# Spreading reciprocals by DMA instead of by matmul, and dividing half of q on GpSimd, in a fused linear-attention and mixture-of-experts kernel

## The reference

```python
qp = _phi(proj(Wq, bq)); kp = _phi(proj(Wk, bk)); v = proj(Wv, bv)     # _phi(x) = elu(x) + 1
# for every token t, in order:
kv   = kv + outer(k_t, v_t)            # per head, 32 x 32
ksum = ksum + k_t                      # per head, 32
num  = q_t @ kv
den  = dot(q_t, ksum) + 1e-6           # one number per token and head
out  = num / den                       # then out @ Wo.T + bo, added to x
```

## Time and profile before

| | us |
|---|---|
| median of 3 runs (lowest to highest) | 1915.71 (1914.94 to 1915.79) |
| the profiled execution, its own time | 1916.06 |
| its span, first to last instruction | 1914.3 |
| PE busy | 1890.7 (99%) |
| weight loads busy, beside PE | 1659.6 (87%) |
| DVE busy | 1569.2 (82%) |
| POOL busy | 889.8 (46%) |
| ACT busy | 663.8 (35%) |
| DMA queue of the program, share of 16 engines | 35.4% |

### The profile page before, as it was taken

One profiled execution on the slowest core, in us unless ns is written; L12 is line 12 of the kernel. 1 busy time (PEld: TensorE's weight loads), 2 busy tenths in 40 slices (PEclk: granted clock), 3 DMA queues, 4 the chain that ended last, 5 costly groups with the idle time before them and its releaser, 6 DMA issues.

```text
span 1914.3 us, 60181 instructions
## 1 busy us (share of the span) xinstructions
PE 1890.7 (99%) x25412; PEld 1659.6 (87%) x25412; DVE 1569.2 (82%) x3356; ACT 663.8 (35%) x1298; POOL 889.8 (46%) x981
## 2 busy tenths in 40 slices
PE   7999999999999999999999999999999999999997
PEld 6888888888888888888888888888888888888887
DVE  7888787888879888778878888887888897888888
ACT  4333333323333332333333433333333333323331
POOL 4345554455443554534554445544345553455422
PEclk9999999999999999999999999999999999999999
DMA  6343234333243432343323334333443234333222
GB/s 215 101 128 112 96 106 128 118 118 112 90 127 119 127 121 74 123 125 116 123 89 118 117 112 136 100 98 113 128 128 112 85 114 130 117 117 113 89 73 90
DMA packets 171197, 217.97 MB, mean 114 GB/s; under 512 B 24368, under 2 KB 85808, under 8 KB 170928
## 3 DMA queue, kind: packets, MB, share of 16 engines
q1 hardware_dynamic: 170928, 214.13, 35.4%
HBM read 151.02 MB, written 63.04 MB: 112 GB/s over the span
## 4 chain that ended last, share of the span: by engine, by line
PE 95%; DVE 2%; POOL 1%; DMA 1%; issue 0%; SPq 0%; ACT 0%; POOLq 0%; DVEq 0%
PE ring L684 38%; PE ring L666 36%; PE ring L758 7%; PE num_ps L788 6%; PE num_ps L771 3%; PE num_ps L801 2%; PE ring L730 1%; PE ring L743 1%; DMA v_tok<-in_wv_t 1%; DVE s_mask L973 0%; PE ring L654 0%; DVE stats L1091 0%; DVE den L1220 0%; DVE res L1084 0%; DVE o_lo L1215 0%
## 5 line engine op out<-in xcount | busy, mean ns | idle before, releaser
L1315 POOL TENSOR_TENSOR k_sum<-k_sum,q_raw 128x512 f32<-128x512 f32 x128 | 165.3, 1291 | 545.0 <-DVE q_raw L984 545.0
L883 ACT ACTIVATE e_tmp<-ring,bias_n 128x512 f32<-128x512 f32 x256 | 175.9, 687 | 509.3 <-PE ring L666 508.7
L973 DVE TENSOR_TENSOR s_mask<-ring,causal 128x512 f32<-128x512 f32 x512 | 315.0, 677 | 0.0
L684 PE MATMUL ring<-wv_hi,xt_hi 128*128 128x260 f32 x1024 | 298.9, 292 | 0.0
L684 PE MATMUL ring<-wv_hi,xt_lo 128*128 128x260 f32 x1024 | 289.2, 282 | 0.0
L684 PE MATMUL ring<-wv_lo,xt_hi 128*128 128x260 f32 x1024 | 289.2, 282 | 0.0
L684 PE MATMUL ring<-wo_hi,o_hi 128*128 128x260 f32 x1016 | 284.8, 281 | 1.3 <-ACT o_hi L938 1.3
L684 PE MATMUL ring<-wo_lo,o_hi 128*128 128x260 f32 x1016 | 285.7, 282 | 0.0
L684 PE MATMUL ring<-wo_hi,o_lo 128*128 128x260 f32 x1016 | 285.5, 284 | 0.2 <-DVE o_lo L1215 0.2
L938 ACT ACTIVATE o_hi<-num_ps 128x512 fp32r<-128x512 f32 x127 | 75.8, 597 | 465.9 <-PE num_ps L788 465.9
L666 PE MATMUL ring<-xt_hi,wk_hi 128*128 128x512 f32 x512 | 207.2, 405 | 3.4 <-DVE xt_lo L1042 1.7
(11 more groups left out here) (147 smaller groups left out, 3955.4 us busy)
## 6 DMA issues: line engine op xcount, KB each, us to landing
x_tok<-in_x SPq DMA_DIRECT2D x128, 256.0 KB, 3.8
res<-in_x SPq DMA_DIRECT2D x128, 256.0 KB, 2.8
out<-res SPq DMA_DIRECT2D x128, 256.0 KB, 2.1
x_in<-in_x_t SPq DMA_DIRECT2D x124, 256.0 KB, 4.7
keys_turned<-k_turned SPq DMA_DIRECT2D x112, 256.0 KB, 2.0
k_tok<-keys_turned SPq DMA_DIRECT2D x448, 64.0 KB, 2.1
x_rows<-moments_rows SPq DMA_DIRECT2D x31, 512.0 KB, 3.6
k_t<-in_wk_t SPq DMA_DIRECT2D x4, 256.0 KB, 4.5
```

Of the source, the lines that this page charges most:

```text
L684: mm = pe.matmul(bank[:, 0:HW], rows[a](k), w[b][:, k, h, :], start=n == 0, stop=n == 3 * KD - 1)
L883: act.activation(e_tmp[:, m], bank, ACT.Relu, bias=bias_n[:, m, g:g + 1], scale=-1.0).then_inc(phi_relu.handle, 1)
L973: dve.tensor_tensor(s_mask[:, j], ring[:, st.bank(u)].rearrange("p (g t) -> p g t", g=KD), repeat(causal, KD), ALU.mult).then_inc(free[st. ...
L1315: pool.tensor_tensor(k_sum[:, g], k_sum[:, g], q_raw[:, g], ALU.mult).then_inc(prod.handle, 1)
```

## The change

- The denominators (`denominators`) are 16 products of 128 columns (four quarters of the tokens, four groups) into 128 partitions of 128 columns. PE does them in tile 2 before L788 instead of after it. ACT's copy and DVE's reciprocal come before o_hi and o_lo.
- The spreading matmuls are gone, with `spread`, the high and low parts of the reciprocal, their copy on ACT and their combination on DVE. Instead, SP stores the reciprocals (64 KB) to DRAM, and eight DMAs of 128 KB each fetch them spread over 32 partitions each into k_sum, four issued by SP (two before and two behind the key fetches of tile 3) and four by ACT.
- `divide` is two instructions of 1024 columns, each from SBUF (k_sum and q_raw): tokens 0 to 255 on DVE at the start of tile 3, tokens 256 to 511 on POOL in tile 3 after the bias row and before `gate_in`. PE waits for the first before the scores of tile 0, for the second before those of tile 2. DVE waits for the second before it writes k_sum and q_raw of the next block.
- Statistics of tile 2's result come directly after its outputs, ahead of the division.
- The ring loses its four R uses and two of three empty ones: 42 uses instead of 48.
- The expert choice gets two buffers of its own (`choice`), and its wait on ACT goes.

```diff
-SKIPS = {0: 1, 3: 2}
+SKIPS = {3: 1}
...
-        uses += [("O", (c, 0)), ("O", (c, 1))] + [("R", g) for g in range(KD)] * (c == 2)
+        uses += [("O", (c, 0)), ("O", (c, 1))]
...
+    def spread_reciprocals(eng, b, heads, *halves):
+
+        eng.wait_ge(den_out.handle, 16 * (b + 1))
+        for half in halves:
+            t = slice(half * BT // 2, (half + 1) * BT // 2)
+            for j in heads:
+                pieces = slice((2 * j + half) * TPB // 2, (2 * j + half + 1) * TPB // 2)
+                rows = den_dram[:, pieces, :].rearrange("g s t -> g (s t)").unsqueeze(0)
+                eng.dma_start(k_sum[j * HD:(j + 1) * HD, :, t], rows.to_broadcast([HD, KD, BT // 2])
+                              ).then_inc(den_in[half].handle, 16)
+
+    def divide(eng, st, half):
+
+        eng.wait_ge(den_in[half].handle, 16 * HPG * (st.off + 2))
+        t = slice(half * BT // 2, (half + 1) * BT // 2)
+        eng.tensor_tensor(q_div[:, (st.off + 1) % 2, :, t], k_sum[:, :, t], q_raw[:, :, t], ALU.mult
+                          ).then_inc(divided[half].handle, 1)
...
+        def send_reciprocals(b):
+            sp.wait_ge(den_rec.handle, b + 1)
+            sp.dma_start(den_dram.rearrange("g r t -> (g r) t"), den).then_inc(den_out.handle, 16)
...
                 if c == 2:
                     send_keys(t, 3)
+                    if st.has("proj"):
+                        send_reciprocals(t + 1)
+                        spread_reciprocals(sp, t + 1, (0, 1), 0)
                     fetch_keys(t, 3)
+                    if st.has("proj"):
+                        spread_reciprocals(sp, t + 1, (0, 1), 1)
...
-            for g in range(KD):
-                for s in range(2):
-                    mm = pe.matmul(bank[g * HD:(g + 1) * HD, 0:BT // 2], head_cols[:, s],
-                                   k_sum[:, g, s * BT // 2:(s + 1) * BT // 2], start=s == 0, stop=s == 1,
-                                   tile_position=(0, g * HD))
+            for s in range(TPB):
+                for g in range(KD):
+                    mm = pe.matmul(bank[g * HD:(g + 1) * HD, 0:P], head_cols[:, s],
+                                   k_sum[:, g, s * P:(s + 1) * P], start=s == 0, stop=s == TPB - 1,
+                                   skip_group_check=True, tile_position=(0, g * HD))
...
+            if c % 2 == 0:
+                pe.wait_ge(divided[c // 2].handle, off + 1)
             for g in range(KD):
-                if c == 0:
-                    pe.wait_ge(free[BANK[("R", g)]].handle, st.freed(("R", g)))
...
                     from_state(st, c)
                     add_state(st, c)
+                    if c == 2 and proj:
+                        denominators(st)
                     from_tile(st, c)
...
-                if c == 2 and attn and proj:
-                    spread_reciprocals(st)
...
-                if c == 2 and proj:
-                    act.wait_ge(den_rec.handle, den_rec.at(st.lin(1, st.off + 1, 1)))
-                    act.activation(rden_high, den, ACT.Copy).then_inc(rden_hi.handle, 1)
+                if c == 2 and attn and proj:
+                    spread_reciprocals(act, st.off + 1, (2, 3), 0, 1)
...
                 if last and proj and attn:
-                    divide(st)
-                if last and attn and proj:
-                    residual_moments(st, 2)
+                    divide(dve, st, 0)
...
-                if c == 2 and proj:
-                    dve.wait_ge(rden_hi.handle, rden_hi.at(st.lin(1, st.off + 1, 1)))
-                    dve.scalar_tensor_tensor(rden, rden_high.bitcast(F32), lo_rows, den,
-                                             ALU.mult, ALU.add).then_inc(rden_parts.handle, 1)
...
                 if last and proj:
+                    divide(pool, st, 1)
                     gate_in(st)
```

More of the change, by code:

```diff
@@ L781, in from_tile @@
                 pe.wait_ge(free[BANK[masked_last]].handle, st.prev.freed(masked_last))
+                if st.off == 0:
+                    masked_last = scores_of(c)[-2]
+                    pe.wait_ge(free[BANK[masked_last]].handle, st.prev.freed(masked_last))
             last = st.alone() and c == TPB - 1
@@ L838, in body @@
                     scores(st, st.off + 1, 0)
-                if last and not attn:
-                    spread_reciprocals(st)
                 if proj:
@@ L930, in body @@
                     exponential(act, 4)
+                if c == 2 and proj:
+                    u = ("DEN", 0)
+                    act.wait_ge(full[st.bank(u)].handle, st.filled(u))
+                    act.activation(den, ring[:, st.bank(u), 0:P], ACT.Copy, bias=DEN_EPS
+                                   ).then_inc(free[st.bank(u)].handle, 1)
                 if st.alone() and last:
@@ L969, in _, with mask_scores @@
     def _(dve):
-        def mask_scores(st, c):
-            for j, u in enumerate(scores_of(c)):
+        def mask_scores(st, c, order=range(HPG)):
+            for j in order:
+                u = scores_of(c)[j]
                 dve.wait_ge(full[st.bank(u)].handle, st.filled(u))
@@ L983, in phi @@
             out = k_t[:, par, g] if m else q_raw[:, g]
+            if kind == "Q" and g == 0 and st.has("attn"):
+                dve.wait_ge(divided[1].handle, st.off + 1)
             dve.scalar_tensor_tensor(out, bank, bias[:, m, g:g + 1], e_tmp[:, m], ALU.add, ALU.max).then_inc(free[st.bank(u)].handle, 1)
@@ L991, in key_sums @@
             dve.wait_ge(free[BANK[("K", g)]].handle, st.freed(("K", g)))
+            if g == 0 and st.has("attn"):
+                dve.wait_ge(divided[1].handle, st.off + 1)
             start = 0.0 if par == 0 else k_carry[:, g:g + 1]
@@ L1024, in turn_keys, with invert @@
                           ).then_inc(keys_turned.handle, 1)
-        def divide(st):
-            for g in range(KD):
-                u = ("R", g)
-                dve.wait_ge(full[st.bank(u)].handle, st.filled(u))
-                bank = ring[:, st.bank(u)]
-                dve.tensor_tensor(q_div[:, (st.off + 1) % 2, g], bank, q_raw[:, g], ALU.mult).then_inc(free[st.bank(u)].handle, 1)
+        def invert(st):
+            dve.wait_ge(free[BANK[("DEN", 0)]].handle, st.freed(("DEN", 0)))
+            dve.reciprocal(den, den).then_inc(den_rec.handle, 1)
         def normalise_first(c):
@@ L1201, in body @@
                     split_x_low(st, 1)
+                if last and not attn:
+                    divide(dve, st, 0)
                 if c == 2 and attn:
@@ L1217, in body @@
                     sum_state(st, c)
-                if c == 2 and proj:
-                    dve.wait_ge(free[BANK[("DEN", 0)]].handle, st.freed(("DEN", 0)))
-                    dve.reciprocal(den, den).then_inc(den_rec.handle, 1)
                 if not last and attn:
```

75 lines of the change are left out of this document (19 added, 56 removed).

## The result

The changed kernel takes 1958.95 us, median of 4 runs (1953.49 to 1968.25); the kernel before, on the same chip, takes 1915.75 (1914.94 to 1916.4). The ratio is 1.0231, with a 95% interval of 1.0191 to 1.027: slower, as forecast (whether by more than 2% the interval leaves open). The forecast was 1966, inside 1900 to 1985. The profiled execution took 1959.86 us (span 1957.8), 43.8 more than that of before, where the sum said 50.1.

The account below looks back on a forecast made before the run. PE's instruction stream was taken to set the time, with DVE's queue 0.67 us from late. The profiled 1916.06 us plus 50.1 (PE's -0.60 a block included) minus 0.35 to the runs' median gave 1966 us, range 1900 to 1985.

Parts of the forecast that it names:

- the 0.67 us of slack: DVE's queue in tile 3: last xt_lo ends at 938.74, PE starts the next block's K projection at 939.41.
- Step on PE: Spreading matmuls leave PE (0.64 us a block), smaller denominator products add 0.04: net -0.60 in each of 32 blocks, -19.2 us.
- Step on DVE and ACT: DVE has less to do, its new multiplication taking 1.22 us and the reciprocal about 0.9; ACT's four DMA issues stay hidden.
- Step on the DMAs: Spreading DMAs: first half lands by about 927 to 927.5, second by 929.5, both before they are wanted; keys in time.
- The step that decides: Tile 3: POOL's multiplication (2.48 us) gets in before DVE's second xt_lo, so K starts 1.8 us later per block, median +1.95.
- Rule: Shared SBUF port: whoever issues first gets it for its whole instruction, so waiting POOL goes before the second xt_lo; chance 0.56.
- rival (a): DVE keeps the port from one xt_lo to the next, so the change gains: 10 us, 1905.5 us; chance 0.28.
- Its size, 50.1: Sum over blocks: 26 x 1.95 + 4 x 0.15 - 2 x 0.60 = +50.1 us on the profiled execution.
- meeting blocks: Blocks where POOL's multiplication runs ahead of DVE's second xt_lo: 26 forecast, +1.95 us each.
- slips: Blocks where DVE's division goes ahead of POOL's last x_in product, POOL's multiplication behind the second xt_lo: 4, +0.15 us each.
- (b): POOL's multiplication and the xt_lo don't meet, only PE's saving remains: 1896.5 us; chance 0.08.
- (c): Spreading DMAs land late behind 1 MB more traffic per block, DVE starts 2.4 us later: 2005 us; chance 0.06.

Follow-up runs that it names:

- gate_first: Changed kernel with POOL's multiplication of q's second half moved behind the four small gate instructions in tile 3; 1921.4 us, ratio 1.0022.
- calm_seconds: calm with the second halves of all spreading DMAs issued by SyncE behind the key fetch, ACT issuing only two first halves; 1900.3 us, ratio 0.9918.
- calm: gate_first with POOL's two instructions on tile 3's x_in postponed until DVE has made the first two xt_lo; 1907.66 us, ratio 0.9963.
- dve_both: Changed kernel with both halves of q multiplied by DVE, one behind the other, and none by POOL; 1975.2 us, ratio 1.0313.
- after_keys: Changed kernel with tile 3's key fetch issued in front of all spreading DMAs; 1977.46 us, ratio 1.0328.
- calm_keys: calm with tile 3's key fetch issued in front of all spreading DMAs; 1919.65 us, ratio 1.0025.

## Why the prediction was right, and where it was not

*What bounds the kernel, and the 0.67 us of slack:* right. What decides is DVE's queue in tile 3. In gate_first the last xt_lo ends 0.93 us later against PE's tile 3 than in before, and PE waits, 22 times.

*Step on PE, -0.60 a block, -19.2:* right as a price, 0.65 or 0.66 in a block where nothing is late. That calm_seconds' span is also exactly 19.2 shorter is chance: it was its fastest run, and by the medians the gain is 16.9. Wrong was "PE's busy time down by about 19 us in any case": it stayed at 1890.5, and fell by that much only where PE hardly waited.

*Step on DVE and ACT:* the multiplication takes 1.19 alone (1.22 forecast), the reciprocal 0.95 (about 0.9), and ACT's copies and issues never show on the path.

*Step on the DMAs:* half right. The first half was forecast to have landed 8.9 to 9.4 us after the denominators' start (927 to 927.5), and DVE to ask at 10.5. It asks at 10.5, but in the median odd block the last of the first half lands at 10.1. It is late 3 times, 1.9 us in all, so "in time" holds with 0.4 us to spare. The second half was forecast at 11.4 and lands at 13.6 in the median odd block, just ahead of POOL's request near 14. That the keys come in time does not hold: PE waits for them 11 times, 5.1 us. Most of these waits lie in blocks where a later wait sets the end, so they probably cost little here, which no run shows by itself; calm against calm_seconds prices them at 7 to 9 us once the rest is gone. The issues were not the mis-sized term: they begin 5.8 us after the denominators' start (5.1 to 5.3 forecast), and four take 1.80 us in the median, 1.74 forecast. The step gave the fetch no time of its own to land. From its last issue until all four had landed, before took 2.0 us in the median and the changed kernel 4.8, so the keys arrive at 12.7 and PE wants them at 12.5. calm_seconds shows that the second halves beside them are a part of it.

*The step that decides, POOL's product between the two xt_lo:* right in mechanism and nearly in the hand-worked times. In the block shown above, from the second res addition (347.49), the prediction put the second xt_lo's end 8.2 us later and K's start 14.1 later; they come 8.5 and 14.3 later. Rule and rival (a) are told apart: POOL, waiting since the end of the bias row, went before the second xt_lo in all 17 blocks where it was already waiting there. That agrees with the Trainium skill (SBUF — State Buffer, Who interferes with whom), which gives the port to whoever issues first. What the rule as read there leaves open, who is served next when both have more to do, the traces of this case answer: the one that waits. POOL's product itself takes 2.40 us alone (gate_first), where 2.48 was taken.

*Its size, 50.1:* two sizes were off, and in opposite directions, so that the sum came within 6.6 us of the spans' 43.5 partly by luck. First the count: 26 meeting blocks were forecast, 17 came; "slips" were 12 instead of 4. By the forecast's own times the last x_in product would begin 0.4 to 0.5 us before DVE asks (its end at 929.7 to 929.9 less 1.64 of length, against 928.60), and only a run that is 0.6 later would slip. In the trace it begins 0.10 before in the median of the 30 blocks, so that the usual spread of the run puts many on the other side. That spread comes, as in before, from the run's start, which waits for the moments' DMA:

```profile
398.74 1.55 POOL L1296 TENSOR_TENSOR x_in<-x_in,x_rows 128x512 f32<-128x512 f32 x1 [0.52 <-DMA x_rows<-moments_rows]
...
520.68 1.54 POOL L1296 TENSOR_TENSOR x_in<-x_in,x_rows 128x512 f32<-128x512 f32 x1 [0.69 <-DMA x_rows<-moments_rows]
```

The first block is a meeting one (+1.86), the second slips (+0.09). In the first the last x_in product is put down 0.23 us before DVE asks, and goes first; in the second only 0.05 us before, and DVE goes first. The blocks of this trace part at some 0.05 us: in all 17 meeting ones the x_in product is put down at least 0.045 us before DVE asks, in all 12 slipping ones at most 0.046 us before, or after. That 0.17 us of a DMA's landing decides over 2 us is read from the traces; no run moved it on purpose. Second the price: a meeting costs 2.25, not 1.95. Of that 0.14 is the half clock in two of the blocks, and PE loses some 0.15 us more than it waits (below). Third, the first period was forecast at -0.60 and came at +1.0: PE waits 0.7 us there for DVE's product, and the granted clock was half for 3.4 us.

*The rivals:* (a) would have given 1905.5 if DVE kept the port. Its condition is false. Its sum was too low as well: gate_first has the xt_lo lengths that (a) describes and takes 1921. Its -0.25 a block is near what gate_first's least disturbed odd blocks show (-0.15 to -0.21). But most even blocks come out at 0 to +0.3: there K is due 0.30 us earlier, and DVE's queue is only 0.20 shorter, which I never looked at. And ten blocks slip, with +0.1 to +1.1, where I had four. (b), no meeting at all, is what calm_seconds had to be built for: 1896.5 forecast, 1900.3 measured. Of (c) there is little: DVE waits for the first half three times.

## What to carry to other kernels

Before work is moved to an idle engine, look at who shares a port with it in that very stretch, not at its share of the span: the same POOL instruction cost 28 us in one place and nothing a few microseconds later. POOL's old x_in product and bias row cost nothing in before and 11 us or more once DVE's product came beside them. A change that wins on the bounding engine and still loses can hide a gain: here POOL's multiplication, one POOL normalisation and two spreading DMAs, each postponed to where nobody waits for it, turn +2.3% into -0.8%. On a queue with several DMAs, put what is wanted last, last, and count what stands in front by its issue, by what it waits for and by its transfer.

## What the runs showed of the hardware

- DVE with two SBUF inputs and POOL take turns when both have work waiting, one instruction each: x_in product, DVE's product, bias row, xt_lo, POOL's product, xt_lo, with no exception in the 17 blocks. The twelve slipping blocks alternate too, and so do dve_both's two products with the bias row between them.
- The next owner gets in before the recorded end of the last: DVE's 1.19 us product ends 1.08 us after POOL's recorded end. Who goes first is settled at some 0.05 us in this trace: POOL went first in the 17 blocks where its x_in product was put down at least 0.045 us before DVE's request, and DVE in the 12 where it was at most 0.046.
- POOL instructions on SBUF never lengthen masks, o_lo or value tiles, which have one input in PSUM: no mask takes more than 0.69 us in any of the traces, no o_lo more than 0.70.
- A wait costs PE more than its length. The first projection after a wait takes 5.68 us to the next tile instead of 5.54 (gate_first against calm, one odd block of each); its first matmul is put down at 0.50 us instead of 0.39. PE's busy sum is also higher where it waits: 1884.5 in gate_first and 1890.5 in the changed kernel against 1871.8 in calm_seconds, for the same 25668 matmuls. A part is that a recorded wait begins only at the modelled end of the last matmul, 0.16 us after the next would have started, and in the changed kernel some 5 us (an estimate: half of three stretches of 3.41 us) are the half clock. So PE's busy time can't be used to show that work left it.
- The granted clock can fall to half for 3.4 us at a wait of PE of some 2 us. Behind the first block this is seen eight times in the traces, each time at a wait of 1.78 to 2.19 us (2.05 and 1.88 in the changed kernel, 2.19 in calm, 1.78 to 1.94 in after_keys). Other waits, up to 1.87 us, didn't bring it.
- With four fetches of 64 KB in front of two spreading DMAs on one queue, these were issued 1.7 us later and landed 3.7 us later (medians of the odd blocks, calm_keys against calm), up to 4.5 us behind DVE's request. The four issues alone take 1.75 us.
